# Two-layer graph kernel: edges cast and turned by DMA, two steps share one take, all rest masks on VectorE

## What is computed

```python
h = relu(layernorm(x)); x = x + neighbour_max(h, adj)      # layer 0: for each node, the maximum of each feature over its neighbours
h = relu(layernorm(x)); x = x + gat(h, adj, W, a)          # layer 1: graph attention
# gat: hw = h @ W; e = leaky_relu((hw@a1)[:,None] + (hw@a2)[None,:], 0.2); e = -9e15 where adj == 0
#      elu(softmax(e) @ hw)
```

## Time and profile before

| | |
|---|---|
| runs | median 742.38 us of 3 (742.05 to 742.62) |
| profiled execution | span 753.0 us from first to last instruction (no other time is listed for it) |
| DVE busy | 693.7 us (92%) |
| PE busy | 681.6 us (91%); weight loads 490.6 us |
| ACT busy | 473.1 us (63%) |
| POOL busy | 281.8 us (37%) |
| DMA | 163.07 MB, mean 217 GB/s |

### The profile page before, as it was taken

How to read it: one execution, slowest core, us unless ns; L and a number is a source line. 1 busy time by engine, 2 the same in 40 slices (tenths; PEclk the granted TensorE clock), 3 DMA queues, 4 the chain that set the end, 5 groups by cost and what they waited for, 6 DMA issues and landing times.

```text
span 753.0 us, 14749 instructions
## 1 busy us (share of the span) xinstructions
PE 681.6 (91%) x5560; PEld 490.6 (65%) x5560; DVE 693.7 (92%) x1023; ACT 473.1 (63%) x685; POOL 281.8 (37%) x259
## 2 busy tenths in 40 slices
PE   1788999999999999999999998699999999999994
PEld 1344655555555555555555554498998999999994
DVE  8999999999999999999999999988998999889893
ACT  3888999889898899998999897562433111001000
POOL 0612034434434535444444355441620294134040
PEclk9999999999999999999999999799999999999998
DMA  9999978997888888888888746342531544443400
GB/s 305 310 355 390 344 230 270 303 327 239 268 249 247 273 258 237 272 265 241 261 263 265 246 143 228 103 143 71 187 130 62 219 140 158 156 177 130 165 15 17
DMA packets 63000, 163.07 MB, mean 217 GB/s; under 512 B 6416, under 2 KB 11152, under 8 KB 58832
## 3 DMA queue, kind: packets, MB, share of 16 engines
q1 hardware_dynamic: 53776, 138.75, 54.2%
q0 software_dynamic: 9152, 23.34, 12.1%
HBM read 117.51 MB, written 44.56 MB: 215 GB/s over the span
## 4 chain that ended last, share of the span: by engine, by line
PE 53%; DVE 31%; issue 12%; ACT 2%; DMA 1%; DVEq 0%; another core or an unknown queue 0%; SPq 0%
PE pick_ps L714 23%; DVE acc L867 20%; PE pick_ps L613 17%; DVE rest L1054 5%; PE late_ps L627 4%; PE late_ps L585 4%; PE order_ps L594 2%; PE late_ps L693 1%; PE late_ps L623 1%; DMA best<-x 1%; DVE left L889 1%; ACT depth L403 1%; DVE found L915 1%; PE late_ps L714 1%; PE order_ps L680 1%
## 5 line engine op out<-in xcount | busy, mean ns | idle before, releaser
L867 DVE TENSOR_TENSOR acc<-pick_ps,acc 128x1024 f32<-128x1024 f32 x248 | 302.6, 1220 | 20.9 <-PE pick_ps L613 12.6
L363 POOL DMA_INDIRECT found<-subset_max,tops x192 | 204.4, 1065 | 271.8 <-DVE acc L867 187.5
L1054 DVE SCALAR_TENSOR_TENSOR rest<-depth,curves_sb,stage 128x512 f32<-128x512 f32 x256 | 199.5, 821 | 15.3 <-PE pick_ps L714 3.1
L714 PE MATMUL pick_ps<-keys,rest 128*128 128x129 f32 x1792 | 207.7, 276 | 3.3 <-DVE rest L1054 3.2
L714 PEld LDWEIGHTS pick_ps<-keys,rest 128*128 128x128 f32 x1792 | 204.6, 193 | 7.4 <-DVE rest L1054 5.8
L402 ACT ACTIVATE first<-order_ps 128x1024 f16<-128x1024 f32 x128 | 131.9, 1030 | 39.1 <-PE order_ps L594 33.0
L403 ACT ACTIVATE depth<-order_ps 128x1024 f16<-128x1024 f32 x128 | 131.5, 1027 | 0.0
L613 PE MATMUL pick_ps<-first,h_hi 128*128 128x512 f16 x256 | 97.3, 380 | 17.6 <-DVE acc L867 17.1
L613 PE MATMUL pick_ps<-second,h_hi 128*128 128x512 f16 x256 | 97.2, 380 | 15.2 <-DVE acc L867 14.7
L585 PEld LDWEIGHTS late_ps<-ident_h,stage 128*128 128x128 f16 x1024 | 68.4, 99 | 50.0 <-DMA stage<-adj 12.9
L613 PE MATMUL pick_ps<-first,h_lo 128*128 128x512 f16 x256 | 97.4, 380 | 0.0
(11 more groups left out here) (146 smaller groups left out, 599.9 us busy)
## 6 DMA issues: line engine op xcount, KB each, us to landing
stage<-adj SPq DMA_DIRECT2D x64, 1024.0 KB
edge_units<-edge_t SPq DMA_DIRECT2D x64, 512.0 KB
stage<-edge_units SPq DMA_DIRECT2D x32, 1024.0 KB, 4.8
subset_max<-keys POOLq DMA_DIRECT2D x13, 512.0 KB, 9.0
found<-subset_max,tops POOLq DMA_INDIRECT x192
best<-x SPq DMA_DIRECT2D x4, 512.0 KB, 5.9
subset_max<-x POOLq DMA_DIRECT2D x4, 512.0 KB, 6.6
out<-keys POOLq DMA_DIRECT2D x7, 256.0 KB, 2.8
```

The lines of the kernel that those rows point to most:

```text
L363: nc.gpsimd.indirect_dma_start(found[:, n % NG, s, :], None, subset_max, bass.IndirectOffsetOnAxis(tops[:, n, s:s + 1], 0)).then_inc(gathe ...
L714: last = nc.tensor.matmul(out_ps(q, b), weight[:, n % WEIGHTS, b * P:(b + 1) * P], wh[:, c, :], start=c == 0 and starts(q, b), stop=c == C ...
L867: V.tensor_tensor(acc[:, q % 2, :], pick_ps[k][:, :], acc[:, q % 2, :], ALU.max).then_inc(raised, 1)
L1054: V.scalar_tensor_tensor(out=weight[:, n % WEIGHTS, :], in0=limit[:, q % 4, :], scalar=slope[:, c:c + 1], in1=units[:, m % EDGES, k * TI:( ...
```

## The change

1. **Edges.** `load`, `flip`, `edges` and `keep` go. POOL issues DMAs that read `adj` from DRAM and write it to DRAM as f16 (`cast_piece`: 512 x 512 values, 1.05 MB read, 0.52 MB written; 8 for each tile). SP issues a transposing DMA for every two steps (`turn`, 0.52 MB into one of 8 `turned` slabs). Layer 1 turns its 32 units of 1.05 MB again from the f16 copy (`turn_unit`), in place of the plain loads.
2. **Pairs.** `second` is made for each step alone. In an odd step `rank` adds a matmul pair with `carry_w` times the `second` of the even step before, so that a target with a second pick in the even step gets none in the odd one. One `pick_joint` adds up the second picks of both steps (8 matmuls), and one take empties it: 3 takes in two steps in place of 4. Seconds that this pushes away go to `rest`, so `FETCHES` is 7.
3. **Rests.** All `rests` run on DVE, two steps at once; `later` goes, and so does an additional matmul in every second `digest` (L623).

The diff, cut to its core:

```diff
             def _(sp):
+                def turn(n):
+                    q, u = n // PER_TILE, n % PER_TILE
+                    sp.wait_ge(cast[q % 2][u * CASTS // PER_TILE], 16 * (q // 2 + 1))
+                    if n >= SLABS:
+                        sp.wait_ge(ordered, (n - SLABS + 1) * KEEP)
+                    sp.dma_start_transpose(turned[:, n % SLABS, :].rearrange("p (c t) -> p c t", t=TI),
+                                           adj_h[q * TI:(q + 1) * TI, u * KCOLS:(u + 1) * KCOLS]).then_inc(landed[n % SLABS], 16)
...
             def _(pool):
+                def cast_piece(q, i):
+                    rows, cols = slice(q * TI, (q + 1) * TI), slice(i * N // CASTS, (i + 1) * N // CASTS)
+                    nc.gpsimd.dma_start(adj_h[rows, cols], adj[rows, cols]).then_inc(cast[q % 2][i], 16)
+                for i in range(EARLY):                      # EARLY = 2, CASTS = 8
+                    cast_piece(0, i)
+                for i in range(4):
+                    pool.wait_ge(x_in[i], 16)
+                for i in range(EARLY, CASTS):
+                    cast_piece(0, i)
...
                 for i, (m, part, bit) in enumerate(CHAINS):
                     pool.wait_ge(chained, i + 1)
                     nc.gpsimd.dma_start(subset_rows(m), spare(i % 4)).then_inc(saved[i % 4], 16)
+                    if i < CASTS:
+                        cast_piece(1, i)
+                for i in range(CASTS):
+                    pool.wait_ge(raised, pick_of(len(CHAINS) + i) + 1)
+                    cast_piece(2, i)
                 pool.wait_ge(saved[3], 32)
...
                     for s in range(FETCHES):
                         if n < LAST * ROWS - 1:
-                            pool.wait_ge(raised, 2 * (STEPS + 2 + QUAD * n) + 4 + s)
+                            pool.wait_ge(raised, pick_of(STEPS + 2 + QUAD * n) + 3 + s)
...
+                    if n // ROWS + 3 < TILES:
+                        for i in range(CASTS // ROWS):
+                            cast_piece(n // ROWS + 3, n % ROWS * CASTS // ROWS + i)
...
             def _(act):                                     # select
-                    nc.scalar.activation(first[:, g % 4, :], order_ps[:, :], ACT.Relu, ...)
+                    if g % 2:
+                        nc.scalar.activation(first[:, g % 4, :], order_ps[:, :], ACT.Sigmoid, ...)
                     nc.scalar.activation(depth[:, g % 4, :], order_ps[:, :], ACT.Abs, bias=MARK - MID).then_inc(depth_ready, 1)
+                    if g % 2 == 0:
+                        nc.scalar.activation(first[:, g % 4, :], order_ps[:, :], ACT.Relu, ...)
...
             def _(pe):
+                def rank(g):
+                    if g % KEEP == 0:
+                        pe.wait_ge(landed[g // KEEP % SLABS], 16 * (g // KEEP // SLABS + 1))
+                        pe.wait_ge(depth_ready, g)          # g > 0
+                        pe.wait_ge(first_ready, g)
+                    for c in range(PAIR):
+                        last = nc.tensor.matmul(order_ps[...], order_w[:, :], edge(g)[...], start=True, stop=g % 2 == 0)
+                    if g % 2:
+                        pe.wait_ge(second_ready, g)
+                        for c in range(PAIR):
+                            last = nc.tensor.matmul(order_ps[...], carry_w[:, :], second[:, (g - 1) % 4, ...], start=False, stop=True)
+                    last.then_inc(ordered, 1)
...
                 for g in range(PAIRS):
-                    pick(g, 0)
+                    pick_first(g)
                     if g + 3 < PAIRS:
                         rank(g + 3)
-                    pick(g, 1)
-                    if g + AHEAD < PAIRS:
-                        flip(g + AHEAD)
+                    if g % 2:
+                        pick_joint(g // 2)
                     if g >= 2:
                         digest(g // 2 - 1, g % 2)
...
                 for g in range(PAIRS):                      # DVE
+                    if g % 2 == 0 and g + 2 < PAIRS:
+                        seconds(g + 2)
-                    take(g, 0)
+                    take(pick_of(g))
-                    if g % 4 == 0:
+                    if g % 2 == 0:
                         rests(g // 2)
-                    elif g % 2 and g + 1 < PAIRS:
-                        seconds(g // 2 + 1)
+                    elif g + 2 < PAIRS:
+                        seconds(g + 2)
-                    take(g, 1)
+                    if g % 2:
+                        take(joint_of(g // 2))
                     ...                                     # chain, fold, search, halve_two as before
```

More of the change, by code:

```diff
@@ L598, in pick @@
[L598 to L615 removed]
+                        last = nc.tensor.matmul(order_ps[:, c * TI:(c + 1) * TI], order_w[:, :], edge(g)[:, c * TI:(c + 1) * TI],
+                                                start=True, stop=g % 2 == 0)
@@ new lines, in rank, with pick @@
+                    if g % 2:
+                        pe.wait_ge(second_ready, g)
+                        for c in range(PAIR):
+                            last = nc.tensor.matmul(order_ps[:, c * TI:(c + 1) * TI], carry_w[:, :], second[:, (g - 1) % 4, c * TI:(c + 1) * TI],
+                                                    start=False, stop=True)
+                    last.then_inc(ordered, 1)
+                def pick(n, parts):
+                    if n >= 2:
+                        pe.wait_ge(raised, n - 1)
+                    for c in range(PAIR):
+                        for i, (p, one_hot) in enumerate(parts):
+                            for part, half_h in enumerate((h_hi, h_lo)):
+                                last = nc.tensor.matmul(pick_ps[n % 2][:, c * TI:(c + 1) * TI], half_h[:, p * PAIR + c, :],
+                                                        one_hot[:, c * TI:(c + 1) * TI], start=i + part == 0, stop=i == len(parts) - 1 and part == 1)
+                    last.then_inc(picked, 1)
@@ new lines, in pick_first, with pick_joint @@
+                def pick_first(g):
+                    pe.wait_ge(first_ready, g + 1)
+                    if g < STEPS // 4:
+                        pe.wait_ge(lo_first, 1)
+                    elif g < STEPS:
+                        pe.wait_ge(lo_ready, g * PAIR // EIGHTH - 1)
+                    pick(pick_of(g), ((g % STEPS, first[:, g % 4, :]),))
+                def pick_joint(m):
+                    pe.wait_ge(second_ready, 2 * m + 2)
+                    pick(joint_of(m), [(g % STEPS, second[:, g % 4, :]) for g in (2 * m, 2 * m + 1)])
```

229 lines of the change are left out of this document (78 added, 151 removed).

## The result

The changed kernel takes 837.83 us (median of 5 runs, 825.06 to 880.85) against 742.38. Its runs spread by 7%, where those of the kernel before agree to 0.1%, so the ratio, 1.1186 with a 95% interval of 1.111 to 1.1262, is taken over its two shortest runs, 825.06 and 836.02. It is slower, as forecast, but by 95 us in the medians (88 by the ratio) and not by 34, and it lies above the range of 735 to 830.

The account below looks back on a forecast made before the run. DVE's own instructions were taken to bound the layer 0 step, PE layer 1. Early DMA +29, the longer step loop +4 and layer 1 +1 gave +34 on the median 742.38: 776 us, range 735 to 830.

Parts of the forecast that it names:

- The ring: Layer 0 loop: dependency cycle through PE, DVE and ACT, 6.76 us for two steps, 3.38 for one, however fast DVE is.
- DVE's own 2.90: Layer 0 loop: DVE's instructions alone after the change, 5.8 us for two steps, 2.90 for one; not expected to be the bound.
- Gives nothing back: Layer 0 loop: work removed from ACT (edge copies, `later`) and PE (flips, additional digest matmul) saves no time.
- I put the difference on the median: Whole kernel: forecast +34 us added to the median 742.38, though the traced span was 753.0, 10.6 above it.
- The 3.50 that the ring had to beat: Step loop of the kernel before: 3.50 us a step, from searches of steps 18 and 126, 377.6 us apart.
- Key 8 at 129: First twenty steps: ACT's key 8, waiting for the last table pieces, comes at 129 us in place of 100.
- the 29: First twenty steps: +29 us from 47.7 MB of early DMA at 376 GB/s, bounds +25 and +88, or nothing.
- The seventh gather: Layer 0 loop: released only by the joint take just before its halving; DVE's slack covers most, leaving 0.03 us a step.
- Hidden under the ring: After step 20: two steps' transfers take 4.2 us at 376 GB/s against 7.1, hidden unless the rate falls below 222 GB/s.
- +1, bounds 0 and +5: Layer 1: seventh gather costs 0.96 us more in each of the last five groups, covered by PE's `mix`; put at +1 us.
- casts and turns run below plain rates: Rival, early DMA: at 310 GB/s key 8 comes at 156, at 256 at 188; total 803 to 835 us, chance 0.17.
- the lower end of 747: Whole kernel: fast end of the main forecast's own range, from 389 GB/s and the bare ring; slow end 802 us.

Follow-up runs that it names:

- pairs_early: Change's paired takes and DVE rests, edges as in the kernel before, gathers released two by two from the second take on: 766.8 us, ratio 1.0314.
- early_gathers: Changed kernel with each group's seven gathers released two by two from the second take on, not one by one from the fourth: median 823.0 us.
- tables_first_early: Changed kernel with tile 2's casts moved behind the tables in POOL's queue and gathers released two by two from the second take on: 800.5 us.
- mirror_plain: Changed kernel without transposing transfers: casts write the mirrored block of the symmetric edges and SP loads it plainly: 805.2 us, ratio 1.0829.

## Why the prediction was wrong

**The ring was right.** `rank` of the odd step waits for DVE, the joint pick stands behind the even rank, and this sets 3.33 a step where it was read as 3.38, 3.43 with halvings where it was put at 3.46. DVE's own 2.90 is not reached. "Gives nothing back" holds against the kernel before, where DVE sets the pace, but not inside the paired loop: with the flips and evictions in it a step takes 3.54 (`pairs_early`), without them 3.43.

**"An execution with a span of 753.0 us ... I put the difference on the median" was wrong.** The 3.50 that the ring had to beat is 3.39 in an ordinary execution. Over the 107 steps that is 12 us more loss, and it is why the paired loop loses time even without traffic. The rows that could have told it were there: the earlier trace rows gives late picks of 10.9 us, near the 10.6 by which the execution was too long.

**"Key 8 at 129 ... That wait is inside the 29, since the sum is one of bytes" failed.** Key 8 came at 152, 52 us late, and for two reasons that are not a sum of bytes.

The first is the order in POOL's queue. The last table pieces stand behind eight casts each of which waits for a take, the last for one of step 18 that ends near 130, and so they leave POOL at 132.65, land 19 us later, and key 8, which every engine needs, comes at 152. The prediction named the casts "before the last table pieces" and did not read their waits. With the block moved key 8 comes at 131.6, and the time falls by about 18 us (825 and 836 to 812).

The second is the slabs. The first search, which needs no table, is 26 to 37 us late in every kernel with all casts and turns, but for `early_gathers` (46), close to the 29 of the sum; but that is luck. It is late because PE waits for slabs: in `tables_first_early` 22 us of such waits lie ahead of it and it is 28 late (of the first slab's wait only what it is longer than that for the first load of before is counted). The turns get only 40 GB/s beside casts. With plain loads of the same edges the first search is 16 us late and no slab but the first is waited for, so one rate for all bytes is not what decides. Alone a turn moved 224 GB/s against 350 for a plain load; the Trainium skill has 261 for one whose middle dimension is not contiguous ("DMA: Bandwidth & Descriptors", section "Latency and other measured facts") and as fast as others ("Advanced Engine Details and Errata", section "X-Bar Transpose (TRN2)"), and the measurement is below both.

**"The seventh gather ... I put 0.03 a step" failed too.** The slack that was to cover it is on the wrong side: the last gather of a group is released by the ninth take after the first pick of its group's step in both kernels, which was 4.5 steps later and is 6 now, and the halving that needs it follows 1.8 us behind its issue. With plain edges the term is not far off: the wait of 1.7 us in 8 steps costs 6.1 us in the loop, 0.06 a step. Where casts and turns keep the gather back, releasing it earlier took 0.15 a step off the loop (3.57 to 3.42) and 16 to 20 us off the time (811.8 and 812.3 to 791.9 and 795.8), and in the longest execution a single wait reached 17.8 us.

**"Hidden under the ring; that cover is gone below 222 GB/s".** On the mean it held: 42 us of engine time a tile against 53, and with the gathers early the step loop ran at 3.42 beside casts and turns, 3.43 without them. It did not hold as a promise for each transfer: with the engines at work all the time a gather or a slab waits in line, and in some stretches the rate fell below 140 GB/s.

**Layer 1, "+1, bounds 0 and +5".** Turned units were never waited for. But the last gathers, released late, came late at the layer's start: 225 to 230 us after the last search in place of 218, and 218.7 to 223.1 with the gathers early. As released in the change the term is +7 to +12, outside its bounds.

The sum as measured, in medians and shortest runs: late tables 18, late gathers 16 to 20, and about 50 that stay in `tables_first_early` (790.1 against 739.9). Of these 28 are the first search, 8 the second, 5 lie after the last search, and 9 are left for the loop. The parts are differences of single edits, and with the few runs of kernels that spread by several per cent they are sure to a few us at best. The rival "casts and turns run below plain rates", 803 to 835 with a chance of 0.17, came nearest, in the time and with key 8 at 156; the low rate is there for the turns, but 20 us of key 8 are the order in the queue. In the forecast's own range the lower end of 747 does not follow from its terms: 742 + 25 - 13 is 754. Nothing hangs on it.

None of the kernels beats the kernel before. Even with the traffic gone and the ring cut the time is 758.7.

## What to carry to other kernels

When a loop gets shorter in instructions, look at what is released by their count: the same nine takes are 6 steps instead of 4.5 when three takes replace four, and the last gather then has no time left. A transfer that stands behind a waiting instruction in a queue is late by that wait, not by its bytes; read every wait ahead of it. When two queues are full at once, count packets before you count bytes: here each got as many packets as the other, and the one with short packets a fifth of the bytes. And before a pace is compared with a forecast, see that the traced execution is as long as the timed ones; a few per cent in the span can be the whole margin.

## What the hardware showed unexpectedly

The transposing transfer moved 224 GB/s alone, in packets of 252 bytes, where a plain load of the same halves moved 350; beside casts it moved 40 and the casts 156, 196 GB/s written together, with the same number of packets on both queues. In some stretches of 10 to 40 us the rate fell to between 67 and 140 GB/s at an undiminished busy share; in these traces that is seen only where casts and turns ran together, and in `mirror_plain`, which has plain loads in place of turns, no slice of ten microseconds of layer 0 with a share above 1.0 moved less than 209. The cause stays open. The times of one kernel spread by up to 9%, where the kernel before stays within 0.4%.
